# Cross-attention and feed-forward kernel, one core: another order of work in the opening and in batch 0

## The chip, the cores and the metric

The kernel runs on one core of a Trainium2 chip. Its time is the device time of one execution in microseconds (us), taken as the median of three runs. A separate execution, recorded by the hardware profiler, gave the profile and the trace. All of the chip's engines appear below: TensorE (PE in the profile, its weight loads PEld), VectorE (DVE), ScalarE (ACT), GpSimd (POOL) and SyncE (SP, which here only issues DMAs). Each runs its own list of instructions in the order in which the code writes them, and waits on semaphores.

## The reference

For each of 16 batches `x[b]` is 512 rows of 512, `ctx[b]` is 77 rows of 512, all fp32. Cut to what matters:

```python
h   = layernorm(x)                                    # per row
Sim = (h@w1)[:, :, None] + (ctx@w2)[:, None, :] + einsum('bid,bjd->bij', h*w3, ctx) + b_sim
A   = softmax(Sim, axis=2);   hq_hat = A @ ctx
Batt = softmax(max(Sim, axis=2), axis=1);  hc_bar = Batt @ h
x = x + concat([h, hq_hat, h*hq_hat, h*hc_bar]) @ W_qv + b_qv     # W_qv: 2048 x 512
h = layernorm(x)
hid = h @ W1 + b1                                     # W1: 512 x 2048
q   = hid + 0.1 * (cos(th)*wre + sin(th)*wim) * wim * sin(th + 0.1*hid)
x = x + relu(q) @ W2 + b2                             # W2: 2048 x 512
```

## The kernel before

Every product is made in three passes of TensorE (`three`): each operand is split into a high part, rounded to the fast 32-bit format, and a low part, the rest. ScalarE writes the high part (`*_high`), VectorE the low one (`*_low`); the passes are high·high, high·low and low·high. A matmul has 128 rows of weights and 512 moving columns; four chunks of 128 (`c`) and three passes make the 12 matmuls of most groups.

**The batches.** `body(b, ...)` is the feed-forward part of batch b, a loop over 16 tiles `f` of W1 and W2, and woven into it the attention of batch n = b+1. In step f TensorE does `hidden(b, f)` (12 matmuls into a bank of `hid`), then `second(b, f-3)` (12 matmuls into `acc`, from `act`). Between them ScalarE and VectorE turn `hid` into `act`: `phase_and_hidden(f)`, `reduce_phase(f)`, `sine`, `sine_term`, `relu_high`, `relu_low`. The attention of batch n lies at fixed steps: `sim` at f=3, `sim_rows` at 4, `spread_max` at 5, `prob_turn` at 8, `hq_hat(n, 0)` at the end of 9, `products` at 10 (after `hidden(b, 10)` and `hidden(b, 11)`), the transposes `tr_second` at 13 and 14. What `sim` needs is made in f=0 to 2: `center` and `scale` (VectorE) put the layer norm on `full`, which holds the turned x of batch n; `spread_high`/`spread_low` split it into `T`; `g_high`/`g_low` make `gs`. The mean and deviation that `center` and `scale` use come through DRAM: `turn_stats` (TensorE), `stat_rows` (ScalarE), then `spread_stats` (three DMAs on SP into `mean_bc` and `e_bc`). `sim_bias` (ScalarE) adds the column term for `sim_rows`.

**The weights.** In batch 0 alone the tiles of W1, W2 and W_qv are split on the chip: SP loads a raw tile into one of two buffers (`raw_w1_load`, `raw_tile_load`), ScalarE and VectorE split it (`w1_high`, `w1_low` into `w1s`, 4 slots; `tile_high`, `tile_low` into `ws`, 5 slots), and GpSimd stores the split tile to DRAM (`w1_store`, `tile_store`). Later batches load the split tiles from there (`w1_load`, `tile_load`, in `weights`). The raw load of W1 tile f waits until tile f-2 is split.

**The opening.** `attention_first` of each engine does batch 0's attention alone. TensorE fills its gaps there with `multiply(k)`, k = 0 to 9: 128 rows of all contexts times a quarter of W_qv, 12 matmuls each, whose results (`product_add`, `product_copy` and then `product_out`) go to DRAM for all batches. These matmuls read `act` buffers in the trace, since the context rows share its memory (`high_parts`, `low_part`); in the same way `w_sb` is the normalised x and `tmp_w` the similarity. `norm_first` makes the normalised x, `context_high`/`context_low` split the context of the batch.

What sets the order is only this written order, engine by engine; a wait holds everything behind it on its engine. Batches 1 to 15 use the split weights and the same code.

Of the kernel before, what the change touches and what calls it, by code (L numbers as in the profile page):

```python
# [50 lines left out]
def xattn_ffn(nc, x, ctx_rows, w_sim, b_sim, W_qv, b_qv, W1, W2, b2, x_turned, ctx_turned, columns, out):  # L51
# [35 lines left out]
    with ExitStack() as ctx:  # L87
# [247 lines left out]
        def _(sp):  # L335
# [123 lines left out]
            def body(b, par, first, last):  # L459
                n, pn = b + 1, 1 - par  # L460
                for f in range(FT):
                    if f == 0 and not last:
                        ctx_load(n)
                    if first:
                        if 2 <= f < FT - 2:
                            raw_w1_load(f + 2)
                        for p in splits(f, last):
                            if p + 1 < STREAM:
                                raw_tile_load(p + 1)
# [27 lines left out]
        def _(pe):  # L497
# [179 lines left out]
            def attention_first():  # L677
                multiply(0)
                multiply(1)
                multiply(2)  # L680
                pe.wait_ge(s_ident, 1)
# [16 lines left out]
                hq_hat(0, 0)  # L698
                pe.wait_ge(c_out, 4)
                products(0, 0, True)  # L700
                multiply(7)
                turn_stats(1)
                tr_second(0, 0)
                tr_second(0, 1)
                multiply(8)
                tr_second(0, 2)
                tr_second(0, 3)
                multiply(9)
# [50 lines left out]
        def _(sc):  # L759
# [131 lines left out]
            def attention_first():  # L891
# [14 lines left out]
                for t in range(2, RT):  # L906
                    turned_high(0, t, 0, tr1, t1_hi)
                    full_copy(0, t)
                sim_bias(0)
                high_parts(6)  # L910
# [5 lines left out]
                high_parts(7)  # L916
# [18 lines left out]
                nc.scalar.activation(trig[:], arg[:], ACT.Sin).then_inc(s_trig, 1)  # L935
                product_copy(7)
                stat_rows(1)
# [7 lines left out]
            def body(b, par, first, last):  # L945
                n, pn = b + 1, 1 - par
                for f in range(FT):
# [14 lines left out]
                    if first and f < FT - 2:  # L962
                        w1_high(f + 2)
# [15 lines left out]
                    if f == 2:  # L979
                        context_high(n)  # L980
                    if f == 3:
                        sim_bias(n)
# [27 lines left out]
        def _(ve):  # L1010
# [290 lines left out]
            def attention_first():  # L1301
# [12 lines left out]
                context_low(0, range(0, 1))  # L1314
                for t in range(RT):
                    norm_first(t)
                low_part(3)
# [12 lines left out]
                row_max(0)  # L1330
                low_part(6)
                product_add(4)
                probabilities(0)
                whole_max(0)
                prob_low(0)
                row_mean_scale(0)
# [11 lines left out]
                product_add(5)  # L1348
                low_part(7)
# [4 lines left out]
                stats_first(1, 1)  # L1354
                chunk(0, 2)
                first_tile_low(2)
                low_part(9)
                stats_first(1, 2)
                stats_first(1, 3)
# [10 lines left out]
                for t in range(RT):  # L1370
                    turned_low(0, t, 0, t2_hi, t2_lo)
                for half in range(2):
                    center(1, half)

            def body(b, par, first, last):
                n, pn = b + 1, 1 - par
                for f in range(FT):
# [23 lines left out]
                    if first and f < FT - 2:  # L1401
                        w1_low(f + 2)
                    if f == 0 and not last:
# [72 lines left out]
        def _(po):  # L1476
# [24 lines left out]
            def weights(b, f, first, last):  # L1501

                if first and f >= FT - 3:
                    po.wait_ge(w1_st[(f + 3) % NW1], 16 * (FT // NW1))
                if f >= FT - 3 and not last or f < FT - 3 and not first:
                    w1_load(b, f + 3)
                if not first:
                    for p in loads_at(f, last):
                        tile_load(b, p, last)
# [64 lines left out]
            def body(b, par, first, last):  # L1574
                n, pn = b + 1, 1 - par
                for f in range(FT):
                    g = FT * b + f
                    if first and f == 0:
                        w1_store(0)
                        w1_store(1)  # L1580
                    if first and f < FT - 2:
                        w1_store(f + 2)
# [7 lines left out]
                    weights(b, f, first, last)  # L1590
# [4 lines left out]
                if first:  # L1595
                    for s in range(NW2):
                        po.wait_ge(w_st[s], 16 * (STREAM // NW2))
                    for s in range(NW1):
                        po.wait_ge(w1_st[s], 16 * (FT // NW1))
# [39 lines left out]
```

## Time and profile before

| | us |
|---|---|
| three runs | 1972.96, 1974.38, 1977.74 |
| median | 1974.38 |
| the profiled execution's own time | 1976.23 |
| its span in the trace | 1974.4 |
| PE busy in the span | 1946.7 |
| DVE, ACT, POOL busy | 1387.4, 989.3, 389.3 |
| mean granted TensorE clock | 0.996 of full speed |

The span leaves 1.83 us of the execution's own time around it. Busy time of TensorE counts matmuls whose modelled ends overlap the next start, so it says how long the engine had work, not that it ran at its peak.

### The profile page before, as it was taken

Reading aid. Unit: us, or ns where it says so; the run is one execution under the profiler, and the core shown is the slowest. Engines: PE = TensorE matmul, PEld = TensorE weight load, DVE = VectorE, ACT = ScalarE, POOL = GpSimd, SP = SyncE. Lnnn points to the kernel's source line nnn. Section 1 sums busy time; section 2 is a strip of 40 time slices with the busy share of each in tenths; the row PEclk is TensorE's granted clock in tenths of the full one; section 3 lists DMA queues with packets and bytes.
Section 4 is the critical chain, followed back from the end, with each engine's and each line's share of the span. In section 5 each row is a group of like instructions: output and inputs, shape, how many; then the busy total and the mean of one; then the engine's idle time right before and its main releaser. Section 6 shows DMA issues by size and latency. Waiting matters only on the chain.

```text
span 1974.4 us, 24660 instructions
## 1 busy us (share of the span) xinstructions
PE 1946.7 (99%) x8791; PEld 1597.7 (81%) x8791; DVE 1387.4 (70%) x2405; ACT 989.3 (50%) x1676; POOL 389.3 (20%) x834
## 2 busy tenths in 40 slices
PE   7889999999999999999999999999999999999999
PEld 5678788888888888888888888888888888888887
DVE  7777776757767676776767767676776767767554
ACT  5474644636355363654636455363553636446343
POOL 1122212121211212112121121212112121121110
PEclk9999999999999999999999999999999999999999
DMA  8476947667475774847657475774748757475473
GB/s 250 145 264 220 306 147 220 202 190 228 138 237 160 230 216 159 240 132 237 213 175 228 146 222 181 215 223 151 229 136 250 215 166 234 149 220 181 143 218 119
DMA packets 140849, 391.73 MB, mean 198 GB/s; under 512 B 21876, under 2 KB 34856, under 8 KB 138808
## 3 DMA queue, kind: packets, MB, share of 16 engines
q0 software_dynamic: 83568, 304.29, 49.7%
q1 hardware_dynamic: 57016, 85.83, 14.2%
q8 instruction: 71, 1.16, 0.3%
q14 instruction: 50, 0.41, 0.1%
q10 hardware_dynamic: 144, 0.04, 0.0%
HBM read 351.83 MB, written 38.27 MB: 198 GB/s over the span
## 4 chain that ended last, share of the span: by engine, by line
PE 95%; DVE 2%; DMA 1%; ACT 1%; issue 0%; SPq 0%; POOL 0%; DVEq 0%; ACTq 0%; POOLq 0%
PE acc L500 18%; PE acc L502 18%; PE acc L501 18%; PE hid L500 12%; PE hid L502 12%; PE hid L501 12%; PE mis L586 1%; PE mis L509 1%; PE mis L502 1%; PE mis L508 1%; PE acc L509 1%; PE acc L508 1%; PE mis L500 1%; PE mis L501 1%; DMA w_raw<-in_L_ffn_W 0%; DMA w1s<-w1x_dram 0%
## 5 line engine op out<-in xcount | busy, mean ns | idle before, releaser
L500 PE MATMUL hid<-T,w1s 128*128 128x512 f32 x1024 | 404.6, 395 | 9.3 <-DVE w1s L1020 7.5
L500 PE MATMUL acc<-ws,act 128*128 128x512 f32 x1024 | 403.2, 394 | 0.0
L502 PE MATMUL hid<-T,w1s 128*128 128x512 f32 x1024 | 400.2, 391 | 0.0
L501 PE MATMUL hid<-T,w1s 128*128 128x512 f32 x1024 | 399.8, 390 | 0.0
L502 PE MATMUL acc<-ws,act 128*128 128x512 f32 x1024 | 399.8, 390 | 0.0
L501 PE MATMUL acc<-ws,act 128*128 128x512 f32 x1024 | 399.4, 390 | 0.0
L1161 DVE TENSOR_SCALAR kk<-ph 128x512 f32<-128x512 f32 x256 | 108.9, 425 | 331.1 <-ACT ph L842 331.1
L851 ACT ACTIVATE act<-h 128x512 fp32r<-128x512 f32 x256 | 162.0, 633 | 349.4 <-DVE h L1153 328.0
L842 ACT ACTIVATE ph<-hid,hbias 128x512 f32<-128x512 f32 x256 | 175.9, 687 | 286.3 <-PE hid L502 285.9
L1498 POOL DMA_DIRECT2D ws<-w2x_dram x240 | 127.8, 533 | 554.6 <-PE acc L502 545.1
L500 PEld LDWEIGHTS hid<-T,w1s 128*128 128x128 f32 x1024 | 193.1, 189 | 51.7 <-DVE w1s L1020 8.7
L1167 DVE SCALAR_TENSOR_TENSOR act<-h,act 128x512 fp32r<-128x512 f32 x256 | 176.1, 688 | 74.4 <-ACT act L851 73.0
L502 PEld LDWEIGHTS hid<-T,w1s 128*128 128x128 f32 x1024 | 192.9, 188 | 40.9
L502 PEld LDWEIGHTS acc<-ws,act 128*128 128x128 f32 x1024 | 192.6, 188 | 40.6
L501 PEld LDWEIGHTS hid<-T,w1s 128*128 128x128 f32 x1024 | 193.3, 189 | 38.9
L500 PEld LDWEIGHTS acc<-ws,act 128*128 128x128 f32 x1024 | 192.7, 188 | 39.4
L501 PEld LDWEIGHTS acc<-ws,act 128*128 128x128 f32 x1024 | 192.7, 188 | 39.0
L1492 POOL DMA_DIRECT2D w1s<-w1x_dram x240 | 129.6, 540 | 455.3 <-PE hid L502 439.3
L1153 DVE SCALAR_TENSOR_TENSOR h<-ph,camp,h 128x512 f32<-128x512 f32 x256 | 191.0, 746 | 0.0
L845 ACT ACTIVATE h<-hid,cols 128x512 f32<-128x512 f32 x256 | 174.7, 682 | 25.4 <-DVE act L1167 25.4
L1163 DVE TENSOR_TENSOR ph<-ph,kk 128x512 f32<-128x512 f32 x256 | 177.3, 693 | 8.8
L855 ACT ACTIVATE ph<-ph 128x512 f32<-128x512 f32 x256 | 158.2, 618 | 0.5
(179 smaller groups left out, 2730.9 us busy)
## 6 DMA issues: line engine op xcount, KB each, us to landing
w1s<-w1x_dram POOLq DMA_DIRECT2D x240, 512.0 KB, 4.0
ws<-w2x_dram POOLq DMA_DIRECT2D x240, 512.0 KB, 4.6
ws<-wqx_dram POOLq DMA_DIRECT2D x56, 512.0 KB, 3.6
full<-in_x_turned SPq DMA_DIRECT2D x15, 1024.0 KB, 8.0
out_x<-X SPq DMA_DIRECT2D x15, 1024.0 KB, 4.7
X<-in_x SPq DMA_DIRECT2D x14, 1024.0 KB, 7.9
w_raw<-in_L_ffn_W SPq DMA_DIRECT2D x32, 256.0 KB, 4.6
w1x_dram<-w1s POOLq DMA_DIRECT2D x16, 512.0 KB, 3.2
```

What stands on the lines that cost most here:

```text
L500: pe.matmul(dst, w_hi, m_hi, start=start, stop=False)
L501: pe.matmul(dst, w_hi, m_lo, start=False, stop=False)
L502: mm = pe.matmul(dst, w_lo, m_hi, start=False, stop=stop)
L842: nc.scalar.activation(ph[:, f % 2], hid[:, f % 2], ACT.Identity, bias=hbias[:, f:f + 1], scale=HSCALE).then_inc(t_done, 1)
L845: nc.scalar.activation(h2[:, f % 2], hid[:, f % 2], ACT.Identity, bias=b1c[:, f:f + 1], scale=1.0).then_inc(h2_done, 1)
L851: nc.scalar.activation(act[:, f % 4, 0], h2[:, f % 2], ACT.Relu).then_inc(act_hi, 1)
L855: nc.scalar.activation(ph[:, f % 2], ph[:, f % 2], ACT.Sin, scale=TWO_PI_BELOW).then_inc(s_done, 1)
L1153: ve.scalar_tensor_tensor(out=h2[:, f % 2], in0=ph[:, f % 2], scalar=camp[:, f:f + 1], in1=h2[:, f % 2], op0=ALU.mult, op1=ALU.add).then_i ...
L1163: ve.tensor_tensor(ph[:, f % 2], ph[:, f % 2], kk[:], ALU.subtract).then_inc(r_done, 1)
L1167: ve.scalar_tensor_tensor(out=act[:, f % 4, 1], in0=h2[:, f % 2], scalar=0.0, in1=act[:, f % 4, 0].bitcast(F32), op0=ALU.max, op1=ALU.subtract
L1492: po.dma_start(w1s[:, s].rearrange("p a c k -> p (a c k)"), w1x_dram[f % FT].rearrange("p a c k -> p (a c k)")).then_inc(w1_in[s], 16)
L1498: po.dma_start(ws[:, slot_of(p)], tile_source(p, last, w2x_dram, wqx_dram)).then_inc(w_in[slot_of(p)], 16)
```

## The change

The order of work changes in the opening and in batch 0; no product is added or left out but sixteen transposes.

- **W1 three ahead.** `w1_high`, `w1_low` and `w1_store` run on tile f+3 in step f (before: f+2), and tile 2 is split in the opening. `raw_w1_load` runs on tile f+4 from f=0.
- **Opening, VectorE.** `context_low` for the first context stands behind `norm_first`; `row_max`, `product_add(5)`, `low_part(7)` and the statistics of batch 1's x change places.
- **Opening, TensorE.** `multiply(7)`, `(9)` are cut in halves; half of 7 stands between `hq_hat(0, 0)` and the products, and `turn_stats(1)` stands right behind the products.
- **Opening, ScalarE.** `high_parts(6)` and `(7)` stand around `sim_bias(0)`, `stat_rows(1)` ahead of `product_copy(7)`.
- **Batch 0.** `scale(1)` is done at the end of the opening; ScalarE's `sim_bias(1)` stands behind `w1_high` in f=3 and its `context_high(1)` in f=4 (before: f=2); `add_b2` is one tile in each of f=3 to 6.
- **Batch 0's end, GpSimd.** In f=13 to 15 the loads for batch 1 are issued ahead of `tile_store`; the waits for all stores at the end of the batch become waits ahead of single loads.
- **Warm-up.** TensorE does 16 transposes of the identity into `hid` before `multiply(0)`.

```diff
@@ SP
-                        if 2 <= f < FT - 2:
-                            raw_w1_load(f + 2)
+                        if f < FT - 4:
+                            raw_w1_load(f + 4)
@@ TensorE, attention_first
+                pe.wait_ge(s_ident, 1)
+                for k in range(16):
+                    pe.transpose(hid[:, 0, 0:P], ident[:], ident[:])
                 multiply(0)
...
                 hq_hat(0, 0)
+                multiply(7, range(0, 2))
                 pe.wait_ge(c_out, 4)
                 products(0, 0, True)
-                multiply(7)
                 turn_stats(1)
+                multiply(7, range(2, C))
+                multiply(8)
                 tr_second(0, 0)
                 tr_second(0, 1)
-                multiply(8)
+                multiply(9, range(0, 2))
                 tr_second(0, 2)
                 tr_second(0, 3)
-                multiply(9)
+                multiply(9, range(2, C))
@@ ScalarE
+                high_parts(6)
                 sim_bias(0)
-                high_parts(6)
+                high_parts(7)
...
+                w1_high(2)
+                stat_rows(1)
                 product_copy(7)
-                stat_rows(1)
...
-                    if first and f < FT - 2:
-                        w1_high(f + 2)
+                    if first and f < FT - 3:
+                        w1_high(f + 3)
+                    if first and f == 3:
+                        sim_bias(n)
...
-                    if f == 2:
+                    if f == (4 if first else 2):
                         context_high(n)
-                    if f == 3:
+                    if f == 3 and not first:
                         sim_bias(n)
@@ VectorE, attention_first
-                context_low(0, range(0, 1))
                 for t in range(RT):
                     norm_first(t)
+                context_low(0, range(0, 1))
...
-                row_max(0)
                 low_part(6)
                 product_add(4)
+                row_max(0)
+                low_part(7)
                 probabilities(0)
                 whole_max(0)
                 prob_low(0)
+                product_add(5)
...
+                turned_low(0, 1, 0, t2_hi, t2_lo)
+                w1_low(2)
+                turned_low(0, 2, 0, t2_hi, t2_lo)
...
                 for half in range(2):
                     center(1, half)
+                for half in range(2):
+                    scale(1, half)
@@ VectorE, body
-                    if first and f < FT - 2:
-                        w1_low(f + 2)
-                    if f == 0 and not last:
+                    if first and f < FT - 3:
+                        w1_low(f + 3)
+                    if f == 0 and not first and not last:
                         scale(n, 0)
...
-                    if f == 3:
-                        add_b2(b, 0)
-                        add_b2(b, 1)
-                    if f == 4:
-                        add_b2(b, 2)
-                        add_b2(b, 3)
+                    if first and 3 <= f < 3 + RT:
+                        add_b2(b, f - 3)
+                    if not first and f in (3, 4):
+                        add_b2(b, 2 * f - 6)
+                        add_b2(b, 2 * f - 5)
@@ GpSimd, body
+                    if first and f >= FT - 3:
+                        weights(b, f, first, last)
...
                         for p in splits(f, last):
                             tile_store(p)
...
-                    weights(b, f, first, last)
+                    if not first:
+                        weights(b, f, first, last)
```

On TensorE the row of 16 stands ahead of the first group of the opening, and a further group of six matmuls (`hid<-T,act`, half of `multiply(7)`) stands between the two products that read `hqs`:

```order
@@ -1,3 +1,4 @@
 L496 UNCONDITIONAL_BRANCH
+L680 MATMUL hid<-ident 128x128 x16
 L500 MATMUL acc<-T,act 128x512
 L501 MATMUL acc<-T,act 128x512
@@ -110,4 +111,10 @@
 L508 MATMUL mis<-at_s,hqs 128x512
 L509 MATMUL mis<-at_s,hqs 128x512
+L500 MATMUL hid<-T,act 128x512
+L501 MATMUL hid<-T,act 128x512
+L502 MATMUL hid<-T,act 128x512
```

The six matmuls came from `multiply(7)`, which stood behind the products as a whole.

VectorE in the opening, before: the context's low part (`hqs`) stands ahead of the four rows that normalise x (`w_sb`).

```order
L1094 TENSOR_TENSOR vareps_x<-row_x,eps_t 128x4
L1020 TENSOR_TENSOR act<-ph,act 128x512
L1020 TENSOR_TENSOR hqs<-ctx_raw,hqs 77x512
L1055 TENSOR_SCALAR w_sb<-X,row_x 128x512 x4
L1020 TENSOR_TENSOR act<-ph,act 128x512
```

VectorE in the opening, of the change (its lines are 7 higher):

```order
L1101 TENSOR_TENSOR vareps_x<-row_x,eps_t 128x4
L1027 TENSOR_TENSOR act<-ph,act 128x512
L1062 TENSOR_SCALAR w_sb<-X,row_x 128x512 x4
L1027 TENSOR_TENSOR hqs<-ctx_raw,hqs 77x512
L1027 TENSOR_TENSOR act<-ph,act 128x512
```

The four rows of x now go first; the low part of `multiply(3)`'s rows (the last row) stays behind both.

ScalarE in batch 0 from step 2's work on `hid` to `sim_bias` (`tmp_w<-mis,vj`), before: four casts of the context lie between.

```order
L855 ACTIVATE ph<-ph 128x512
L827 CAST ws<-w_raw 128x512
L819 CAST hqs<-ctx_raw 128x512
L820 CAST hqs<-ctx_raw 39x512
L819 CAST hqw<-ctx_raw 128x512
L820 CAST hqw<-ctx_raw 39x512
L842 ACTIVATE ph<-hid,hbias 128x512
L845 ACTIVATE h<-hid,cols 128x512
L835 CAST w1s<-w_raw 128x512
L851 ACTIVATE act<-h 128x512
L855 ACTIVATE ph<-ph 128x512
L827 CAST ws<-w_raw 128x512
```

The same stretch of the change:

```order
L859 ACTIVATE ph<-ph 128x512
L831 CAST ws<-w_raw 128x512
L846 ACTIVATE ph<-hid,hbias 128x512
L849 ACTIVATE h<-hid,cols 128x512
L839 CAST w1s<-w_raw 128x512
L864 ACTIVATE tmp_w<-mis,vj 77x512
L855 ACTIVATE act<-h 128x512
L859 ACTIVATE ph<-ph 128x512
L831 CAST ws<-w_raw 128x512
```

`sim_bias` moved up over the casts of the context and over three rows of its own step; the casts stand two steps later.

## Rows read from the trace of the kernel before

**Rows 1.** The page, part 4: the chain that ended last, by engine.
```profile
PE 95%; DVE 2%; DMA 1%; ACT 1%; issue 0%; SPq 0%; POOL 0%; DVEq 0%; ACTq 0%; POOLq 0%
```
**Rows 2.** Waits of PE, whole span: us in total, times, longest.
```profile
PE acc L500 <- DVE act L1020: 7.8, 2, 7.0
PE hid L500 <- DVE w1s L1020: 7.5, 2, 3.9
...
PE mis L586 <- DVE w_sb L1055: 2.0, 1, 2.0
...
PE hid L500 <- DMA w1s<-w1x_dram: 1.8, 1, 1.8
```
**Rows 3.** Windows: length, busy time by engine, PEclk, DMA share, GB/s.
```profile
20.00:30.00 10.00, 9.19 (x40) 7.03 (x39) 8.35 (x17) 4.62 (x9) 1.71 (x2) 0.83 0.64 187
...
90.00:100.00 10.00, 8.66 (x30) 6.28 (x31) 7.98 (x17) 8.14 (x18) 1.60 (x3) 0.83 0.54 181
...
140.00:160.00 20.00, 16.05 (x63) 12.76 (x63) 14.30 (x25) 9.40 (x17) 2.54 (x5) 0.91 0.63 236
```
**Rows 4.** Timeline of DVE in the opening: start, us, instruction, [idle before].
```profile
18.24 0.69 DVE L1020 TENSOR_TENSOR hqs<-ctx_raw,hqs 77x512 fp32r<-77x512 f32 x1 [4.91 <-ACT hqs L820]
18.85 1.91 DVE L1055 TENSOR_SCALAR w_sb<-X,row_x 128x512 f32<-128x512 f32 x4
```
**Rows 5.** Timeline of PE in the opening.
```profile
9.73 0.63 PE L500 MATMUL acc<-T,act 128*128 128x512 f32 x1
10.15 0.63 PE L501 MATMUL acc<-T,act 128*128 128x512 f32 x1
...
13.76 0.39 PE L502 MATMUL acc<-T,act 128*128 128x512 f32 x1
13.98 0.39 PE L500 MATMUL acc<-T,act 128*128 128x512 f32 x1
...
21.41 0.53 PE L500 MATMUL acc<-T,act 128*128 128x512 f32 x1 [0.81 <-DVE act L1020]
```
**Rows 6.** Timeline of PE at the start of batch 0's products.
```profile
40.58 0.47 PE L508 MATMUL mis<-at_s,hqs 128*128 128x512 f32 x1 [0.38 <-DVE hqw L1020]
...
44.48 0.50 PE L500 MATMUL acc<-w0s,T 128*128 128x512 f32 x1 [0.88 <-DVE w0s L1020]
```
**Rows 7.** Timelines of ACT, DVE, ACT and PE: from `stat_rows(1)` to `sim(1)`.
```profile
70.76 0.25 ACT L772 COPY mean_bc<-mis 12x128 f32<-12x128 f32 x1
...
78.22 2.36 DVE L1040 TENSOR_TENSOR full<-full,mean_bc 128x1024 f32<-128x1024 f32 x2 [1.30 <-DMA e_bc<-stat_dram]
...
83.36 2.48 DVE L1046 TENSOR_TENSOR full<-full,e_bc 128x1024 f32<-128x1024 f32 x2
...
86.91 0.68 ACT L842 ACTIVATE ph<-hid,hbias 128x512 f32<-128x512 f32 x1
...
90.10 0.79 PE L500 MATMUL hid<-T,w1s 128*128 128x512 f32 x1 [3.59 <-DVE w1s L1020]
...
95.90 0.42 PE L500 MATMUL mis<-T,gs 128*77 128x512 f32 x1 [1.24 <-DVE T L1020]
```
**Rows 8.** Timelines of ACT, DVE and PE in steps 2 to 8 of batch 0.
```profile
99.08 0.62 ACT L819 CAST hqs<-ctx_raw 128x512 fp32r<-128x512 f32 x1
...
122.53 0.69 ACT L842 ACTIVATE ph<-hid,hbias 128x512 f32<-128x512 f32 x1
...
128.87 0.68 DVE L1167 SCALAR_TENSOR_TENSOR act<-h,act 128x512 fp32r<-128x512 f32 x1
...
106.53 0.48 PE L615 MATMUL mis<-ident,tmp_w 77*128 77x77 f32 x4 [2.23 <-ACT tmp_w L860]
...
131.57 0.48 PE L500 MATMUL acc<-ws,act 128*128 128x512 f32 x1
```
**Rows 9.** Timelines of PE and POOL: W1 tile 11, and batch 1's W1 tile 1.
```profile
147.41 0.50 PE L500 MATMUL hid<-T,w1s 128*128 128x512 f32 x1 [3.95 <-DVE w1s L1020]
...
204.11 0.54 POOL L1492 DMA_DIRECT2D w1s<-w1x_dram  x1
```

More of the change, by code:

```diff
@@ L680, in attention_first @@
                 multiply(2)
-                pe.wait_ge(s_ident, 1)
                 tr_first(0, 0)
@@ L915, in attention_first @@
                 stack_out(0)
-                high_parts(7)
                 product_copy(6)
@@ L1347, in attention_first @@
                 first_tile_low(0)
-                product_add(5)
-                low_part(7)
                 chunk(0, 1)
@@ L1354, in attention_first @@
                 stats_first(1, 1)
+                stats_first(1, 2)
+                stats_first(1, 3)
                 chunk(0, 2)
@@ L1357, in attention_first @@
                 low_part(9)
-                stats_first(1, 2)
-                stats_first(1, 3)
                 chunk(0, 3)
@@ L1369, in attention_first @@
                     norm_second(0, t)
-                for t in range(RT):
-                    turned_low(0, t, 0, t2_hi, t2_lo)
+                turned_low(0, 0, 0, t2_hi, t2_lo)
+                turned_low(0, 1, 0, t2_hi, t2_lo)
+                w1_low(2)
+                turned_low(0, 2, 0, t2_hi, t2_lo)
+                turned_low(0, 3, 0, t2_hi, t2_lo)
                 for half in range(2):
                     center(1, half)
+                for half in range(2):
+                    scale(1, half)
             def body(b, par, first, last):
@@ L1504, in weights @@
                     po.wait_ge(w1_st[(f + 3) % NW1], 16 * (FT // NW1))
+                if b == 1 and f == 0:
+                    po.wait_ge(w1_st[3], 16 * (FT // NW1))
                 if f >= FT - 3 and not last or f < FT - 3 and not first:
@@ L1508, in weights @@
                     for p in loads_at(f, last):
+                        if b == 1 and p < NW2:
+                            po.wait_ge(w_st[slot_of(p)], 16 * (STREAM // NW2))
                         tile_load(b, p, last)
@@ L1578, in body @@
                     if first and f == 0:
[L1579 to L1582, printed above, removed]
+                        for k in range(3):
+                            w1_store(k)
+                    if first and f < FT - 3:
+                        w1_store(f + 3)
+                    if first and f >= FT - 3:
+                        weights(b, f, first, last)
                     if first and 3 <= f < 3 + CN - GAP:
@@ L1594, in body @@
                         deviation_second(n)
[L1595 to L1599, printed above, removed]
             batches(po, attention_first, body, lambda: None)
```

## The prediction

> **What bounds the kernel now.** First the chain that ended last: 95% of it is TensorE [rows 1]. A change of order can therefore win only time in which TensorE stands still or runs at the low clock. Then TensorE's waits [rows 2]: leaving out the 7.0 us before its first matmul, they are 0.8 us (acc, in the opening), 7.5 us in two waits for W1 tiles (3.9 and, as the rest, 3.6), 2.0 for the normalised x, 1.8 for a W1 tile from DRAM, and by the timeline 2.23 for the similarity's bias [rows 8], 1.24 for the turned x of batch 1 [rows 7], 0.38 and 0.88 at the first products [rows 6]: about 17 us, all before 214 us. The fourteen batches behind these have none, and nothing of theirs is changed. Then the clock: after a wait the granted clock fell to 1.2 GHz. A window of 10 us that shows 0.83 has lost 10 x 0.17 = 1.7 us [rows 3]; so have 90 to 100 us, and 140 to 160 (20 x 0.09 = 1.8). The same fall follows the wait of 2.23; the waits of 1.24 and 1.8 have none. With the slow start (below) about 9 us go to the clock. So at most 26 us can be won, of 1974.4.
>
> From here "TensorE is at -3" means that it does the same matmuls 3 us earlier than before.
>
> **1. The opening: -3.35.** Before, VectorE waited 4.91 us for the context's high part, and only then normalised x, for 1.91 us [rows 4]; TensorE waited 2.0 for it, then 0.81, and `multiply(3)` began at 21.41 [rows 5] at the low clock. Now x goes first, in the wait. The low part that `multiply(3)` needs stays behind the context's, whose end is set by a DMA, so it comes 1.91 us earlier and no more: 19.5 in place of 21.4. With the fall of the clock gone (part of 1.7) the next bound is the chain similarity, row maximum, softmax, `context_low`, at about -2.3; it has `product_add(4)`, `low_part(7)` and `product_add(5)` in it, 0.6 each on VectorE, of which one had been there and two fall into VectorE's waits for TensorE and ScalarE. The products' start at 44.48 [rows 6] so comes to -2.0, and half of `multiply(7)`, six matmuls of 0.23 (13.98 less 13.76 [rows 5]) = 1.36, has been done by then in what was the wait of 0.88 and the gap ahead of it. Behind the products TensorE is at -3.35. If the clock falls in the gap before 19.5 it is -2.65; if the softmax chain is not delayed, -4.
>
> **The warm-up: 0.** `multiply(0)` ran at 0.43 us per matmul (10.15 less 9.73 [rows 5]) and not at 0.23; ten of them cost 2.0. But `multiply(3)` cannot begin before 19.5, by VectorE and a DMA, whether TensorE is done with `multiply(2)` at 17.4 or at 16. So the 2.0 are not on the path. The transposes stand before the first matmul's 7.0 and delay nothing. On the clock: TensorE had transposes in the gap 17.6 to 21.4 and the clock still fell [rows 3, 5]. The Trainium skill says (TensorE: Matmul & The Clock Gate, Part 4: PE-mode transpose) that transposes do not count as activity for the full clock; by that the warm-up changes nothing, without it `multiply(0)` is fast and then waits longer, which may cost the fall priced above. The one sum is -3.35, the other -2.65; this trace agrees with the rule as far as it goes.
>
> **2. Hidden tile 3 and sim(1): 0 more.** Tile 3 is now split a step earlier, and the wait of 3.59 at 90.10 [rows 7] goes. What is late next is `sim(1)`, which stood 1.24 behind it. Its chain: `stat_rows` at 70.76, the three DMAs, `center` at 78.22, 7.5 us later, then `scale` (2.48) behind step 0's work of VectorE, the high parts, ScalarE's step 1 from 86.91, `g_high`, the last low parts, 95.90. Now `turn_stats` stands ahead of `multiply(7)` instead of behind it, and ScalarE copies at 65.9; the DMAs, 7.5, end at 73.4, when VectorE is still at `turned_low` until 74.3. `center` then takes 2.4, `scale` 2.5, to 79.1; `reduce_phase(0)` waits behind that (1.1, to 80.2), `sine`, two high parts of 0.5, and ScalarE's step 1 begins at 81.9 in place of 86.91: -5.0. From there the chain is what it was: `sim(1)` at 90.8. TensorE ends `hidden(3)` at 86.5 - 3.35, and 2.7 for twelve matmuls: 85.9. It waits 4.9 us, longer than any wait before, and the clock falls, 1.7. -5.1 + 1.7 = -3.4: the wait of 3.6 has become one in front of `sim(1)`. Bounds: no fall -5.1; a chain that gains only as much as TensorE, -1.7.
>
> **3. The similarity's bias: -3.95.** `sim_rows` waited 2.23, and the clock fell [rows 8]. `sim_bias` loses four casts ahead of it (0.62 each from 99.08) and three rows of its own step, and now follows `w1_high` as soon as `sim` ends, a `second` and a `hidden` (5.5 us) before it is needed. 2.23 + 1.7 = 3.95: TensorE at -7.35. Bounds 2.2 to 4.
>
> **4. Steps 5 to 9: +3.1.** ScalarE and VectorE don't follow that far. Before, `second(5)` began at 131.57, 2.0 us behind the end of `relu_low(5)` at 129.55 [rows 8]. ScalarE's step 4 now begins when `hidden(4)` ends (before, at 106.53 - 2.23 = 104.3 [rows 8]; less 3.4 it is 100.9); the casts of the context, 2.6 us, come behind it, in front of the two changes of activation table. Followed through, step 6 begins on ScalarE at 117.8 in place of 122.53 (-4.7), and VectorE has one more `add_b2` (0.6) in it: `relu_low(5)` ends at 125.4, -4.15. TensorE, at -7.35, is there at 124.2 and waits 1.2; then about 1 more for `relu_low(6)` and for the high part of `at_s` in front of `hq_hat(1, 0)`. It leaves step 9 with the chain: -4.25. These waits are each as short as the 1.24 and 1.8 that left the clock alone. Bounds: 1.2 if only the first is real; 5 if the clock falls once.
>
> **5. W1 tile 11: -5.1.** The wait of 3.95 at 147.41 [rows 9] was for a raw tile that SP had issued behind the 1 MB load of x; then 1.8 of clock. It is now issued two steps earlier, ahead of that load: 5.75 gone. What comes next is `add_first_part`, which must empty `acc` before the products: by VectorE at -4.15 its last tile ends at 144.4, and TensorE loses 0.6. -9.35. Tile 13 is now the one issued behind the load of x; by the chain it is wanted some 13 us after its issue. Bounds 4 to 5.8.
>
> **6. Batch 1's second W1 tile: -1.8.** Its load was issued at 204.11 behind a `tile_store` [rows 9]; now it stands one store earlier, some 7 us. The wait of 1.8 goes: -11.15. `tile_load(1, 0)` stands ahead of the last store and waits for `second(11)`, which ends before that store's tile is split. Bounds 0 to 1.8.
>
> **The sum.** 3.35 + 0.05 + 3.95 - 3.1 + 5.1 + 1.8 = 11.15. The profiled execution of 1976.23 (span 1974.4 and 1.83 around it) comes to 1965.1; it stands 1.85 above the median of the runs, and from 1974.38 the sum gives **1963.2 us**.
>
> **Rivals.**
> A. The sim wait does not come. If VectorE and ScalarE keep pace better than the hand-made chain above (steps 2 and 4), the clock stays up and the waits of 3.1 halve: 1.7 + 1.5 + 0.5 = 3.7 more, 1959.5. For it: every term there is a chain of small latencies that I took from crowded rows. Against: `center` can't start before 73.4 and 4.9 us of VectorE follow it.
> B. The change does not split far ahead. There are still two raw buffers, so raw tile f+4 waits for the split of f+2; if tile 11 still comes late, its 5.1 stay: 1968.3. Against: step 8 needs only the split of tile 9, in step 6, and x is loaded behind it.
> C. ScalarE and VectorE set the pace in steps 4 to 9 with a further fall of the clock and short waits in each step, 3.5 us worse than in 4: 1966.7. For it: six instructions of 0.5 to 0.7 us per step on each, at 5.5 us per step of TensorE.
> D. Slower. `w1_high(2)` now stands ahead of `stat_rows(1)` on ScalarE and waits for a raw tile that SP issues behind the 1 MB of turned x. If it lands d us after 65.8, `turn_stats`'s copy, the second transpose of `tr_second`, `center` and all behind it come later by d. From d = 11.2 the kernel is slower; at d = 14 it takes 1977. Against: before, the DMA engines had both raw tiles moved in about 5 us after their issue.
>
> **How the numbers follow.** Forecast 0.50 (own range 1960.5 to 1966); A 0.18; B 0.08; C 0.18; D 0.03; 0.03 for something unseen without a gain. The range of 8 in 10 takes in A and C and part of B: 1957.5 to 1970. About 0.3%, 5.9 us, is what a measurement of this kernel can tell from no change, so faster means under 1968.5: the forecast, A, most of C and half of B, 0.86; within it 0.10; slower 0.04.
>
> **What would show it.** No wait in front of `hidden(3)` and one of 4 to 5 us in front of `sim(1)`, with PEclk near 0.8 behind it; no wait for the bias; short waits for `relu_low` or `at_s` in steps 8 and 9; none for tile 11 nor for batch 1's loads; the products of batch 0 from about 42.5 us. The prediction is wrong if TensorE waits for `hidden(11)` or for `stat_rows`, if a new wait lies in batch 1 or later, or if step 9 ends less than 3 us ahead of before.

## The result, and the profile after

| | median us | lowest to highest | runs |
|---|---|---|---|
| before | 1974.49 | 1972.96 to 1977.74 | 9 |
| after | 1969.31 | 1968.84 to 1971.65 | 9 |

The ratio is 0.9974, with a 95% interval of 0.9966 to 0.9982: the change makes the kernel 5.2 us faster, 0.26%. Forecast were 11.15 us. The sign was right and the time lies in the range, but the size was more than twice what came, and by the forecast's own bound for "faster", 1968.5, the result falls in the outcome that it gave 0.10. The profiled execution of after took 1970.50 with a span of 1968.7 (before 1976.23 and 1974.4), at a mean granted clock of 0.996 in both.

First, after's waits of TensorE over the whole span: engine, buffer and line, what it waited for, then us in total, times, longest.

```profile
PE mis L500 <- DVE T L1027: 4.6, 1, 4.6
PE acc L500 <- DVE act L1027: 3.7, 2, 1.9
PE mis L615 <- ACT tmp_w L864: 1.9, 1, 1.9
PE acc L500 <- DVE act L1174: 1.7, 2, 1.0
```

The two waits for `w1s` that came to 7.5 [rows 2], the one for W1 from DRAM and the 2.23 for the bias [rows 8] are gone. The two that matter are 4.6 in front of `sim(1)`, which was forecast, and 1.9 for `tmp_w` of the opening's softmax, which was not. Their places, in the timeline of TensorE (start, us, instruction, idle before it and its releaser):

```profile
19.75 0.50 PE L500 MATMUL acc<-T,act 128*128 128x512 f32 x1 [1.73 <-DVE act L1027]
...
32.14 0.72 PE L615 MATMUL mis<-ident,tmp_w 77*128 77x77 f32 x4 [1.94 <-ACT tmp_w L864]
39.42 0.30 PE L630 MATMUL mis<-ident,prs 128*128 128x128 f32 x1 [0.58 <-DVE prs L1027]
...
47.00 0.40 PE L500 MATMUL acc<-w0s,T 128*128 128x512 f32 x1
...
79.10 0.47 PE L500 MATMUL hid<-T,w1s 128*128 128x512 f32 x1
...
95.44 0.68 PE L500 MATMUL mis<-T,gs 128*77 128x512 f32 x1 [4.62 <-DVE T L1027]
...
130.64 0.50 PE L500 MATMUL acc<-ws,act 128*128 128x512 f32 x1 [0.96 <-DVE act L1174]
137.09 0.50 PE L500 MATMUL acc<-ws,act 128*128 128x512 f32 x1 [0.71 <-DVE act L1174]
140.99 0.50 PE L508 MATMUL mis<-at_s,hqs 128*128 128x512 f32 x1 [0.89 <-ACT at_s L885]
...
221.17 0.40 PE L500 MATMUL mis<-T,gs 128*77 128x512 f32 x1
```

The same matmuls of before that neither the rows nor the prediction show: `hidden(0)`, `hq_hat(1, 0)` and batch 1's similarity.

```profile
77.99 0.39 PE L500 MATMUL hid<-T,w1s 128*128 128x512 f32 x1
...
139.95 0.50 PE L508 MATMUL mis<-at_s,hqs 128*128 128x512 f32 x1
...
227.22 0.40 PE L500 MATMUL mis<-T,gs 128*77 128x512 f32 x1
```

`multiply(3)` is 1.66 earlier (21.41 [rows 5]), as forecast. But the first product of batch 0 is 2.5 later (44.48 [rows 6]), and `sim(1)` only 0.46 earlier (95.90 [rows 7]). `hidden(0)` began at 77.99 and begins at 79.10: +1.1, where -3.35 was forecast. From there on the change gains: batch 1's similarity comes 6.05 earlier. So the later stages gained 7.15, for which the forecast had 7.8. The 4.45 between -3.35 and +1.1 are the miss, and they lie before 47 us.

The windows of after (length; busy time of PE, PEld, DVE, ACT, POOL; PEclk; DMA share; GB/s) show them too:

```profile
30.00:40.00 10.00, 7.48 (x33) 5.78 (x33) 5.95 (x14) 4.36 (x10) 1.30 (x2) 0.83 1.06 388
...
90.00:100.00 10.00, 5.38 (x15) 3.16 (x14) 7.99 (x17) 7.46 (x16) 1.75 (x4) 0.68 0.55 191
...
140.00:160.00 20.00, 18.97 (x80) 14.56 (x80) 17.59 (x30) 10.42 (x19) 3.20 (x6) 1.00 0.75 280
```

The fall at 20 to 30 us is gone [rows 3] and there is one at 30 to 40, where before had 1.00. The fall behind tile 11's wait is gone, the one at 90 to 100 is deeper.

What held the opening back is on ScalarE (same columns):

```profile
30.89 0.62 ACT L793 CAST act<-ph 128x512 fp32r<-128x512 f32 x1 [6.14 <-DMA ph<-in_ctx_turned]
31.41 0.68 ACT L864 ACTIVATE tmp_w<-mis,vj 77x512 f32<-77x512 f32 x1
35.31 0.62 ACT L793 CAST act<-ph 128x512 fp32r<-128x512 f32 x1 [3.22 <-DMA ph<-in_ctx_turned]
35.84 0.46 ACT L869 ACTIVATE prob<-prob 128x308 f32<-128x308 f32 x1
```

The casts (L793) are `high_parts(6)` and `(7)`. Each waits for a raw tile of context rows, and what is queued behind it is on the softmax chain: `sim_bias(0)` behind the first, the exponentials behind the second. Before had the first behind `sim_bias` (L860, at 31.13) and the second behind the softmax, and neither waited:

```profile
31.72 0.61 ACT L789 CAST act<-ph 128x512 fp32r<-128x512 f32 x1
...
39.45 0.62 ACT L789 CAST act<-ph 128x512 fp32r<-128x512 f32 x1
```

And these are the issues of the two tiles in after, on SP:

```profile
21.09 0.55 SPq L362 DMA_DIRECT2D ph<-in_ctx_turned  x1
...
24.19 0.36 SPq L369 DMA_DIRECT2D hqw_dram<-X  x1
24.59 0.60 SPq L362 DMA_DIRECT2D ph<-in_ctx_turned  x1
```

"Row 6" and "row 7" below stand for the 128 context rows each that `multiply(6)` and `multiply(7)` use. Each load stands behind a `product_out` (`hqw_dram<-X`; that of row 6 is issued at 20.71), which waits for a sum of VectorE. From issue to cast it is 9.8 us for row 6 and 10.7 for row 7, and by the trace the loads took just as long to land; the DMA share was 0.82 at 20 to 30 us and 1.06 at 30 to 40.

### The profile page after: what moved, and what is told of

Read it like the earlier page. It is cut to its first block, busy times and chain, and to the rows that moved or that the text cites. A ratio compares the mean times of both kernels' runs of the same rounds, so it can differ in the third digit from the quotient of the medians.

```text
span 1968.7 us, 24691 instructions
## 1 busy us (share of the span) xinstructions
PE 1948.3 (99%) x8807; PEld 1598.2 (81%) x8807; DVE 1387.2 (70%) x2405; ACT 988.9 (50%) x1676; POOL 389.4 (20%) x834
## 3 DMA queue, kind: packets, MB, share of 16 engines
q0 software_dynamic: 83568, 304.29, 49.6%
## 4 chain that ended last, share of the span: by engine, by line
PE 92%; DVE 3%; ACT 2%; DMA 1%; issue 1%; SPq 0%; DVEq 0%; ACTq 0%
PE acc L500 17%; PE acc L502 17%; PE acc L501 17%; PE hid L502 11%; PE hid L500 11%; PE hid L501 11%; PE mis L586 1%; PE acc L508 1%; PE acc L509 1%; PE mis L508 1%; PE mis L509 1%; PE mis L500 1%; PE mis L502 1%; PE mis L501 1%; DMA ph<-in_ctx_turned 1%
```

## The experiments

Each was compared with runs of before on the same chip. Differences below are against that before. The places in the traces come from one profiled execution of each kernel: the four kernels that share the whole opening of "rows early" (bias late, context in f=3, second(0) first, GpSimd as before) and that kernel itself have `hidden(0)` between 74.48 and 74.83, so a difference of less than 0.4 us in that column means nothing.

| kernel | median us | before | ratio, 95% | TensorE at `hidden(0)` |
|---|---|---|---|---|
| after | 1969.31 | 1974.49 | 0.9974 (0.9966 to 0.9982) | 79.10 (before 77.99) |
| softmax order undone | 1967.41 | 1975.76 | 0.9956 (0.9943 to 0.9968) | 75.72 |
| rows early | 1965.96 | 1975.76 | 0.9949 (0.9937 to 0.9962) | 74.48 |
| no transposes | 1968.83 | 1975.76 | 0.9967 (0.9954 to 0.9979) | 78.36 |
| 26 transposes | 1969.68 | 1975.76 | 0.9969 (0.9957 to 0.9981) | 79.91 |
| rows early, W1 two ahead | 1972.28 | 1975.40 | 0.9983 (0.9974 to 0.9992) | 74.73 |
| rows early, bias late | 1963.67 | 1975.40 | 0.9942 (0.9928 to 0.9955) | 74.83 |
| rows early, context in f=3 | 1963.41 | 1975.40 | 0.9944 (0.9932 to 0.9956) | 74.55 |
| the same, second(0) first | 1963.90 | 1975.40 | 0.9944 (0.9932 to 0.9956) | 74.72 |
| before, rows early | 1975.15 | 1975.62 | 0.9997 (0.9988 to 1.0006) | 78.39 |
| rows early, GpSimd as before | 1967.62 | 1975.62 | 0.9951 (0.9939 to 0.9964) | 74.80 |
| context in f=3, no transposes | 1964.15 | 1975.62 | 0.9936 (0.9922 to 0.9949) | 74.95 |

### The opening: softmax order undone

`high_parts(6)`, `(7)`, `low_part(7)`, `product_add(5)` and `row_max` stand as in before, and `multiply(7)` is whole again behind the products (behind `turn_stats(1)` too, which stays where the change put it); all else is after.

```diff
@@ ScalarE
-                high_parts(6)
                 sim_bias(0)
-                high_parts(7)
+                high_parts(6)
...
+                high_parts(7)
@@ TensorE
-                multiply(7, range(0, 2))
...
-                multiply(7, range(2, C))
+                multiply(7)
@@ VectorE
+                row_max(0)
...
-                row_max(0)
-                low_part(7)
...
-                product_add(5)
...
+                product_add(5)
+                low_part(7)
```

> The changed kernel with one part undone: high_parts(6) and (7), low_part(7), product_add(5), row_max and multiply(7) stand in the opening where they stood before. Theory (the raw context rows 6 and 7 come late, and the moved high_parts wait for them in front of sim_bias and of the softmax): the waits of 6.1 and 3.2 us of ScalarE for the rows go, batch 0's products start at about 42.5 us instead of 47.0, hidden(0) at about 76 instead of 79.1, and the kernel takes about 1966 us. Rival (the extra VectorE work in the softmax chain costs the time, three instructions of 0.6): the products start no earlier than 45, and the kernel takes about 1968. Rival (the warm-up is at fault): no change, 1969.3.

It took 8.35 us less than before, against 5.2 for after: this part of the change costs more than it brings. TensorE has no wait for `tmp_w`; only the small ones of before are left [rows 6], and `hidden(0)` comes at -2.3:

```profile
38.23 0.47 PE L508 MATMUL mis<-at_s,hqs 128*128 128x512 f32 x1 [0.38 <-DVE hqw L1026]
42.13 0.50 PE L500 MATMUL acc<-w0s,T 128*128 128x512 f32 x1 [0.87 <-DVE w0s L1026]
```

### The opening: rows early

This keeps the new order whole and takes away what makes the casts wait: SP issues both rows' loads ahead of the two `product_out`.

```diff
@@ SP
                 rows_in(5)
-                product_out(0)
                 rows_in(6)
+                rows_in(7)
+                product_out(0)
...
                 product_out(1)
-                rows_in(7)
```

> The changed kernel with one thing more: SP issues the loads of the raw context rows 6 and 7 ahead of the first product_out instead of behind it and behind the waits for the stored products. No order on ScalarE, VectorE or TensorE is touched. Theory (late rows): they land before they are wanted, the products start at about 42.5 us and the kernel takes about 1965 us, 4.4 less than the changed kernel. Rival (VectorE work in the chain): the products start at 45 to 46, 1968. Rival (DMA bandwidth in 20 to 40 us is full, so that rows early only delay something else that is wanted as early): a new wait of the same size elsewhere in the opening, 1968 to 1970.

9.8 us less than before. SP's timeline (both rows are in the group that begins at 13.58, ahead of the first `product_out`; row 7 goes out at 19.3, when its buffer is free), and then ScalarE's:

```profile
13.58 6.25 SPq L362 DMA_DIRECT2D ph<-in_ctx_turned  x2
20.29 0.34 SPq L369 DMA_DIRECT2D hqw_dram<-X  x1
```

```profile
28.43 0.69 ACT L864 ACTIVATE tmp_w<-mis,vj 77x512 f32<-77x512 f32 x1 [3.59 <-PE mis L502]
29.02 0.61 ACT L793 CAST act<-ph 128x512 fp32r<-128x512 f32 x1
```

The cast, that of row 7, runs without a wait, and `sim_bias(0)` ahead of it waits for TensorE alone. The exponentials begin at 31.44, against 35.84 in after. TensorE's timeline:

```profile
42.39 0.40 PE L500 MATMUL acc<-w0s,T 128*128 128x512 f32 x1
...
74.48 0.47 PE L500 MATMUL hid<-T,w1s 128*128 128x512 f32 x1
...
90.82 0.68 PE L500 MATMUL mis<-T,gs 128*77 128x512 f32 x1 [4.60 <-DVE T L1027]
...
125.06 0.50 PE L500 MATMUL acc<-ws,act 128*128 128x512 f32 x1 [0.97 <-DVE act L1174]
131.50 0.50 PE L500 MATMUL acc<-ws,act 128*128 128x512 f32 x1 [0.71 <-DVE act L1174]
...
215.61 0.40 PE L500 MATMUL mis<-T,gs 128*77 128x512 f32 x1
```

These are the forecast's figures: products from 42.5, `hidden(0)` at 77.99 - 3.35 = 74.6, `sim(1)` at 90.8 behind 4.9 of waiting. At batch 1's similarity TensorE is at -11.6 (forecast -11.15). The 4.6 between after's 47.00 and 42.39 here are 1.94 and 0.58 of waits, 1.7 of clock in the window of 30 to 40 us, and 0.4 that it had gained by `multiply(3)`, 19.32. Against the kernel with the order undone, which ran beside it, it is 1.5 us faster by the medians of five runs each and 1.2 at `hidden(0)`: that is what the reordering brings when its rows have landed.

### The control: before, rows early

The same edit of SP on before.

> The kernel before, with the raw context rows 6 and 7 loaded early and nothing else. Theory (late rows cost only since the change moved high_parts(6) and (7) up; before, ScalarE took them at 31.7 and 39.4 us without a wait): within 1 us of the kernel before. Rival (early rows are a gain of their own, so e2 says nothing of the change): 2 us or more faster.

Ratio 0.9997, 0.9988 to 1.0006: nothing. The early loads bring no time of their own; they are worth something only to an order that wants the rows early.

### The warm-up: none, and 26

```diff
@@ TensorE
                 pe.wait_ge(s_ident, 1)
-                for k in range(16):
-                    pe.transpose(hid[:, 0, 0:P], ident[:], ident[:])
                 multiply(0)
```

> The changed kernel without the 16 transposes in front of multiply(0). Theory (VectorE and DMA set the start of multiply(3), the warm-up is worth nothing): within 1 us of the changed kernel, 1968.5 to 1970.5, multiply(0) at 0.43 us per matmul from the start. Rival (the full clock of the first matmuls is worth its time): 1 to 2 us slower. Rival (the transposes cost a fall of the clock later): up to 1.7 faster.

In the other kernel, `range(26)` stands in place of `range(16)`.

> The changed kernel with 26 transposes in front of multiply(0) instead of 16, so that TensorE has work until about the first matmul. If transposes keep the clock up as the first matmuls of the changed kernel suggest, multiply(0) and (1) run at 0.23 us throughout and no fall shows in 7 to 12 us; multiply(2) still waits for its low part until 13.4 and multiply(3) until 19.7, so the time stays within 1 us of the changed kernel. If transposes do not count, multiply(0) runs at 0.43 us as without a warm-up.

The medians of the three kernels lie within a microsecond; against its own before each is 6.9, 6.1 and (after) 5.2 us faster, with intervals that overlap. So a gain from the warm-up doesn't show, and the kernel without it has the lowest median; a difference of a microsecond either way isn't excluded.

What the transposes do to the clock varies from one profiled execution to the next. After, whose row of 16 ends at about 5.1:

```profile
7.64 0.39 PE L502 MATMUL acc<-T,act 128*128 128x512 f32 x1
7.88 0.39 PE L500 MATMUL acc<-T,act 128*128 128x512 f32 x1
...
8.72 0.63 PE L500 MATMUL acc<-T,act 128*128 128x512 f32 x1
9.15 0.63 PE L501 MATMUL acc<-T,act 128*128 128x512 f32 x1
```

and the kernel with the softmax order undone, with the same 16 transposes in the same place:

```profile
8.12 0.63 PE L502 MATMUL acc<-T,act 128*128 128x512 f32 x1
8.55 0.63 PE L500 MATMUL acc<-T,act 128*128 128x512 f32 x1
```

Read the spacing of the starts. In after the first matmuls follow each other in 0.23 us (2.4 GHz), then, from 8.3 to 11.7, in 0.43 (1.2 GHz). Of the eight kernels with 16 transposes three begin so (after and rows early for five matmuls, second(0) first for fewer); the other five have 0.43 from the first matmul on, for 6 to 14 matmuls. Of the four without transposes none begins at 0.23; they have 0.43 for 10 to 13 matmuls. With 26, `multiply(0)` and `(1)` run at 0.23 but for two matmuls at 0.35. TensorE had done nothing else before. So a row of transposes can bring the clock up; 16 of them did it in three executions out of eight.

With 26 the forecast's other worry came true: `multiply(2)` is done sooner and TensorE waits longer in front of `multiply(3)`.

```profile
19.72 0.50 PE L500 MATMUL acc<-T,act 128*128 128x512 f32 x1 [2.20 <-DVE act L1027]
```

Behind that wait the granted clock falls (0.83 at 20 to 30 us, where after has 1.00), and `hidden(0)` comes at 79.91, against 78.36 without transposes. `multiply(3)` starts at 19.7 to 19.9 in all three.

### W1 two ahead

On the kernel with the rows early, `raw_w1_load`, `w1_high`, `w1_low` and `w1_store` run two ahead as in before.

```diff
@@ SP
-                        if f < FT - 4:
-                            raw_w1_load(f + 4)
+                        if 2 <= f < FT - 2:
+                            raw_w1_load(f + 2)
@@ ScalarE, and VectorE and GpSimd likewise
-                w1_high(2)
...
-                    if first and f < FT - 3:
-                        w1_high(f + 3)
+                    if first and f < FT - 2:
+                        w1_high(f + 2)
```

> The kernel with the rows 6 and 7 loaded early (e2), with the W1 tiles split two ahead again, as before the change; all else as in e2. Theory (step 2 of the prediction: tile 3 a step earlier wins nothing, since sim(1) waits for center, scale and the high parts of ScalarE; step 5: it pays at tile 11 alone): a wait in front of hidden(3) is back, sim(1) still begins at about 91 us, the wait of some 4 us in front of hidden(11) is back with its fall of the clock, and the kernel is about 5 us slower than e2, 5 us faster than before. Rival (the tiles pay at both places): about 8 us slower than e2. Rival (they pay nowhere, since VectorE and ScalarE set the pace): within 1 us of e2.

3.1 us less than before, so 6.7 slower than the same kernel with W1 three ahead (each against its own before), where 5 was expected. TensorE's timeline:

```profile
85.27 0.50 PE L500 MATMUL hid<-T,w1s 128*128 128x512 f32 x1 [1.07 <-DVE w1s L1026]
91.07 0.43 PE L500 MATMUL mis<-T,gs 128*77 128x512 f32 x1 [2.79 <-DVE T L1026]
...
141.60 0.50 PE L500 MATMUL hid<-T,w1s 128*128 128x512 f32 x1 [2.24 <-DVE w1s L1026]
```

`sim(1)` comes at 91.07 against 90.82: three ahead is worth nothing there, it moves a wait for W1 into the wait for the turned x. It pays behind that, but not as expected: the wait in front of tile 11 is 2.24 and not 4, and the clock does not fall behind it (1.00 from 140 to 160 us). The rest lies in short waits and in one of 2.93 in front of `sim(2)`, at 222.63, with a fall of the clock; of it the forecast had nothing, and why `sim(2)` is late there was not followed.

### The bias late

On the kernel with the rows early, `sim_bias(1)` goes back to the end of f=3 and `context_high(1)` to f=2.

```diff
@@ ScalarE, body
-                    if first and f == 3:
-                        sim_bias(n)
...
-                    if f == (4 if first else 2):
+                    if f == 2:
                         context_high(n)
-                    if f == 3 and not first:
+                    if f == 3:
                         sim_bias(n)
```

> The kernel with the rows early (e2), with sim_bias(1) and context_high(1) of ScalarE where they stood before the change (end of f=3, f=2). Theory (steps 3 and 4 together: what the bias wins, ScalarE and VectorE take back in steps 8 and 9 with the context's casts in f=4): the wait of some 2 us for the bias is back with its fall of the clock, the three short waits of steps 8 and 9 are gone, and the kernel is 1 us (0 to 2) slower than e2. Rival (the bias's 3.95 stays won): 4 us slower than e2.

Both were wrong. It took 11.7 us less than before, where the kernel with the rows early took 9.8, and by the trace it gains 1.5 us on that kernel between `hidden(0)` and batch 1's similarity (74.83 to 214.42, so 139.6, where the other has 74.48 to 215.61, 141.1). `sim(1)` waits 4.59 as it did. The wait for the bias in its timeline:

```profile
101.78 0.49 PE L615 MATMUL mis<-ident,tmp_w 77*128 77x77 f32 x4 [0.63 <-ACT tmp_w L864]
...
134.21 0.50 PE L508 MATMUL mis<-at_s,hqs 128*128 128x512 f32 x1 [0.53 <-ACT at_s L885]
```

0.63 in place of 2.23, and no fall of the clock behind it. The two waits for `act` are gone, and 0.53 of the one for `at_s` is left. The bias itself is no earlier: ScalarE writes it 9.9 us behind the start of `sim(1)` in both kernels (91.17 to 101.06 here, 95.90 to 105.80 in before). What changed is TensorE. The clock falls behind the wait of 4.59, so `sim(1)`, `second(0)` and `hidden(4)` take 9.98 us (91.17 to 101.78 less 0.63), where before took 8.40 (95.90 to 106.53 less 2.23). The 1.6 is the fall of step 2, and the bias was late enough to hide it. Moving `sim_bias` and the context can therefore win 0.63 here at most, and the two moves cost more in steps 5 to 9 than that.

### The context in f=3

`sim_bias` stays early and only the four casts go one step up, on the kernel with the rows early.

```diff
@@ ScalarE, body
-                    if f == (4 if first else 2):
+                    if f == (3 if first else 2):
                         context_high(n)
```

> The kernel with the rows early (e2), with the context's four casts of batch 1 at the end of f=3 instead of f=4. In the changed kernel ScalarE was idle 2.8 us there, waiting for hidden(4), and the casts take 2.6. Theory (the casts in f=4 are what makes ScalarE and VectorE late): the waits of 0.97, 0.71 and 0.89 us in steps 8 and 9 go, the kernel is 2 to 2.6 us faster than e2, about 12.4 us faster than before. Rival (VectorE's own instructions set the pace there, add_b2 in f=6 among them): less than 0.7 us faster than e2.

12.0 us less than before, the lowest median measured, though the bias-late kernel lies within 0.3 us of it. The waits of 0.97 and 0.71 for `act` are gone; in front of `hq_hat(1, 0)` 0.72 is left:

```profile
133.65 0.50 PE L508 MATMUL mis<-at_s,hqs 128*128 128x512 f32 x1 [0.72 <-ACT at_s L885]
```

In step 3 ScalarE has the time: it waits 2.79 us at the start of step 4 in after. From step 4 the casts push what follows.

### second(0) ahead of sim(1)

On the last kernel TensorE does `second(0, 0)` first, to fill the wait of 4.6.

```diff
@@ TensorE, body
-                    if f == 3 and not last:
+                    if f == 3 and not last and b > 0:
                         sim(n, pn)
...
+                    if f == 3 and b == 0:
+                        sim(n, pn)
```

> e7 with one thing more: in batch 0 TensorE does second(0) ahead of sim(1) in f=3, in the wait of 4.6 us. act is ready about 2.6 us before T is. Theory (TensorE has nothing else to do there): the wait in front of sim(1) becomes about 2 us in front of second(0), the clock falls at most once, and the kernel is 2.5 to 4.3 us faster than e7. Rival (VectorE and ScalarE, which wait for hid less then, set the pace of f=4 to 9): at most 1 us faster than e7, with longer waits in front of second(4) to second(6).

Nothing: 1963.90 against 1963.41, with intervals that are the same. The wait became three:

```profile
88.47 0.50 PE L500 MATMUL acc<-ws,act 128*128 128x512 f32 x1 [1.99 <-DVE act L1176]
97.54 0.49 PE L615 MATMUL mis<-ident,tmp_w 77*128 77x77 f32 x4 [0.51 <-ACT tmp_w L866]
106.36 0.65 PE L622 MATMUL mis<-ident,rmax 128*128 128x128 f32 x4 [2.81 <-DVE rmax L1188]
```

They add up to 5.3. Around step 3 VectorE's and ScalarE's chain sets the time, wherever TensorE waits for it.

### GpSimd's order at the end of batch 0

On the kernel with the rows early, the loads for batch 1 stand behind `tile_store` again.

```diff
@@ GpSimd, body
-                    if first and f >= FT - 3:
-                        weights(b, f, first, last)
...
-                    if not first:
-                        weights(b, f, first, last)
+                    weights(b, f, first, last)
```

> The kernel with the rows early (e2), with GpSimd's loads for batch 1 behind the tile_stores of f=13 to 15 again, as before the change. Theory (step 6 of the prediction): the wait of 1.8 us in front of batch 1's second hidden is back, and the kernel is 1.8 us slower than e2, some 8 us faster than before. Rival (the wait had gone with the W1 tiles, which are stored a step earlier): within 0.5 us of e2, 9.8 faster than before.

8.0 us less than before, and 1.8 less gained than with the new order. The wait is back, at 0.76 instead of 1.8:

```profile
204.15 0.50 PE L500 MATMUL hid<-T,w1s 128*128 128x512 f32 x1 [0.76 <-DMA w1s<-w1x_dram]
```

Against the other kernel it also has a longer fall of the clock behind `sim(1)`, 0.69 in place of 0.83 at 90 to 100 us, a hundred us ahead of the edit, which is worth up to 1 us. So the part is worth about 0.8 to 1.8, and the rest of the 1.81 that the wait had in before went with the other edits.

### The context in f=3, without transposes

Both edits together, on the kernel with the rows early.

> e7 (rows early, the context's casts at the end of f=3) without the 16 transposes. Theory (the warm-up is worth nothing, on this side as well): within 1 us of e7, 11.5 to 13 us faster than before. Rival (the warm-up pays as soon as the opening has no wait for rows): 2 us slower than e7.

11.5 us less than before, within a microsecond of the same with transposes. No gain from the warm-up shows there either.

## Why the prediction was wrong in size

- **Step 1, the opening: this is the step that failed.** It said -3.35 and +1.1 came. It bounded the softmax chain by VectorE's additions (0.6 each, two of them free) and named no load: the step moved `high_parts(6)` and `(7)` up in ScalarE's queue, each behind a load and ahead of the softmax, and put their waits at nothing without a reason. In before row 6 was issued at 22.75, landed 8.7 us later, at 31.45, and was cast at 31.72: it was just in time. Row 7 had 2.6 us to spare. After the change the casts waited 6.14 and 3.22. The rows-early run shows the rest of the step right (42.39 for the forecast 42.5, and 74.48 for 74.6), and the undone order, -2.3 at `hidden(0)`, shows that the loss lay in this part. The six matmuls of `multiply(7)` and the other gains of the reordering are real: 1.5 by the times. The forecast's sign of being wrong, step 9 less than 3 us ahead of before, came true: `hq_hat(1, 0)` is 1.04 behind.
- **The warm-up: 0, right,** and for the reason given: `multiply(3)` is set by VectorE. The rule that the forecast weighed did not hold in every execution. The Trainium skill (TensorE: Matmul & The Clock Gate, Part 4: PE-mode transpose) has transposes not count for the full clock; here the matmuls behind 16 of them started 0.23 us apart in three executions and 0.43 in five, and those behind none 0.43 in all four. Where the three differ from the page, the measurement decides.
- **Step 2, right.** The wait at `hidden(3)` became 4.62 at `sim(1)` (forecast 4.9), and the clock fell. In the rows-early run, where the opening is as forecast, the chain holds term by term: `center` begins at 74.30 (forecast 74.3), ScalarE's step 1 at 81.83 (81.9), `sim(1)` at 90.82 (90.8). In the W1-two-ahead run `sim(1)` comes at the same time. Rival A, without a sim wait, is out.
- **Step 3, mis-sized: 3.95 forecast, 0.63 at most shown.** The wait and the fall are gone, but the bias-late run had only 0.63 left of them without this edit. The other 1.6 vanished behind the fall that follows the wait for `sim(1)`, and with a wait of 0.63 there was no second fall to save.
- **Step 4, right in kind, 3.1 forecast.** The waits are 0.96, 0.71 and 0.89, together 2.56, and the clock holds, so rival C is out. The context-in-f=3 run shows that the four casts cause most of them. Steps 3 and 4 together were forecast at +0.85; the bias-late run says that without the two moves the kernel is 1.5 (by the trace) to 1.9 us (by the medians, each against its own before) better.
- **Step 5, right in the sum.** No wait for tile 11 and no fall; put back, though, the wait was 2.24 without a fall, and other waits, with a fall at `sim(2)`, made up the 6.7. Rival B is out with it. With step 6, TensorE gained 7.1 between `hq_hat(1, 0)` and batch 1's similarity (1.04 behind before, then 6.05 ahead); 6.9 was forecast.
- **Step 6: 0.8 to 1.8,** forecast 1.8.
- **Rival D** named the kind of failure but at the wrong load. `w1_high(2)` did wait for its tile, 4.57 us, and ended in time: `stat_rows(1)` came at 70.06, after 1.25 more for `turn_stats` (70.76 before).

One thing stays open. From `hidden(0)` to where `second(5)` could start after needs 50.6 us (130.64 - 0.96 - 79.10), the rows-early kernel 49.6 (125.06 - 0.97 - 74.48), with the same wait in front of `sim(1)`. The granted clock at 90 to 100 us is 0.68 in the one and 0.83 in the other; it was 0.69 with GpSimd's order as before and 0.74 with the context in f=3. The fall behind one and the same wait so costs up to 1 us more or less. Nor is the length of the wait enough to say whether there is a fall: behind 1.94 in after there was one, behind 2.24 in the W1-two-ahead run none. What sets it was not tried.

## What to carry to other kernels

When a step moves up in an engine's queue, look for what it reads and when that was issued: a consumer that did not wait in the profile has shown only that it came late enough. Take each DMA behind a moved step from its issue to the first use, at the DMA share of that stretch, and if it is near, move the load along with the consumer. And where an edit removes a wait that stands behind another one, price it in the kernel in which the first has changed: here 1.6 of the 2.23 went without it, because TensorE had become slower by as much.

## What the runs showed of the hardware

- The loads of rows 6 and 7, 256 KB each, took 9.8 and 10.7 us from issue to landing in after, and 8.7 and 10.5 in before. In the rows-early kernel, issued at 13.58 and 19.3, they took 6.7 and 3.2. The view of DMA issues, from 18 to 42 us in after (KB each, median us from issue to landing):

```profile
ph<-in_ctx_turned SPq DMA_DIRECT2D x2, 256.0 KB, 10.2
```

  Over the whole kernel before, the 256 KB loads of `w_raw` had a median of 4.6. In after GpSimd issues two loads of 1 MB at 20.34 and 23.57, next to the two rows; that these make them late is likely, but no run moved them. The Trainium skill (DMA: Bandwidth & Descriptors, Anatomy of one DMA) has, for DMAs that GpSimd issues, about 2.0 us and the bytes at 436 GB/s, which is an estimate of 2.6 us for 256 KB. These are issued by SP. The 3.2 is near it, the 9.8 and 10.7 are not; the sum has no term for other loads under way, and here the measurement decides.
- Transposes of a 128x128 identity can have TensorE's clock at 2.4 GHz for the first matmuls, as told above, and don't do so each time. The PEclk column doesn't show a slow start: without transposes, and in the five executions with 16 that began at 0.43, it stands at 1.00 for the first 10 us. It does show the fall in after (0.92 there). For the start the spacing has to be read.
